# Dummy matrix products on TensorE behind the first transposes and behind the two group sums of a GroupNorm

## What is computed

```
g = x.reshape(B, R, C, 32, 6)
xn = (g - mean(g, (1, 2, 4))) / sqrt(var(g, (1, 2, 4)) + 1e-5)
q0 = xn[:, 0]                                   # first row of each column
sw = softmax over rows of (q0 Wq_s) . (xn Wk_s)
Q = (xn Wq) * scaling * sw ; K = xn Wk ; V = xn Wv
attn = softmax over columns of sum over rows of Q . K
out = x + sum over columns of attn * V
```

## Time and profile before

| | |
|---|---|
| median of 3 runs | 629.26 us (626.15 to 629.93) |
| the profiled execution | 631.34 us, span 629.5 us |
| busy: PE, DVE | 505.7 us (80%), 422.6 us (67%) |
| busy: ACT, POOL | 252.1 us (40%), 225.3 us (36%) |
| mean granted clock of PE | 0.904 |
| DMA | 152.84 MB, mean 243 GB/s |

### The profile page before, as it was taken

The page is one execution under the profiler, slowest core; times in us unless marked ns, Lnnn a source line. Parts: engine busy times, 40 slices in busy tenths (PEclk is TensorE's granted clock), DMA queues, the critical chain, the costliest instruction groups (busy, mean ns, idle before and its releaser), DMA issues.

```text
span 629.5 us, 15205 instructions
## 1 busy us (share of the span) xinstructions
PE 505.7 (80%) x5368; PEld 403.9 (64%) x5368; DVE 422.6 (67%) x1029; ACT 252.1 (40%) x555; POOL 225.3 (36%) x231
## 2 busy tenths in 40 slices
PE   0030198999649999999998999869499997999794
PEld 0020177998525555555546998758399997998683
DVE  2899848699945766767663666846266663667764
ACT  0030136678416666666652113223255652122232
POOL 1010024478503433434341000547166663001484
PEclk9996557799659999999998999979699998999988
DMA  8993004699965998989999999999878757999998
GB/s 275 407 434 163 0 1 118 190 265 273 265 199 165 247 279 247 265 259 246 264 230 194 283 293 279 284 331 263 276 228 263 255 162 158 298 288 283 298 257 227
DMA packets 206876, 152.84 MB, mean 243 GB/s; under 512 B 169648, under 2 KB 189680, under 8 KB 206064
## 3 DMA queue, kind: packets, MB, share of 16 engines
q1 hardware_dynamic: 154912, 132.14, 72.1%
q10 hardware_dynamic: 51920, 20.11, 12.6%
HBM read 95.60 MB, written 56.62 MB: 242 GB/s over the span
## 4 chain that ended last, share of the span: by engine, by line
PE 58%; DVE 18%; DMA 7%; SPq 5%; issue 4%; ACTq 3%; ACT 2%; POOL 2%; POOLq 0%; DVEq 0%
PE PS L990 19%; PE PS L1000 10%; PE PS L1051 7%; DVE EXTRA L603 7%; DVE BIG L849 5%; PE PS L882 3%; PE PS L1080 3%; PE PS L1081 3%; PE PS L1084 3%; PE PS L1082 3%; PE PS L1083 3%; PE PS L921 2%; DMA v_scratch<-EXTRA 2%; DVE EXTRA L709 2%; ACTq L575 2%
## 5 line engine op out<-in xcount | busy, mean ns | idle before, releaser
L449 POOL TENSOR_TENSOR BIG<-EXTRA,BIG 128x192 f32 (+1 forms) x144 | 106.7, 742 | 148.7 <-ACT BIG L519 147.1
L990 PE MATMUL PS<-WP,EXTRA 128*128 128x384 f16 (+1 forms) x1152 | 152.0, 291 | 9.5 <-DMA EXTRA<-xt_scratch 8.7
L990 PEld LDWEIGHTS PS<-WP,EXTRA 128*128 128x128 f16 x1152 | 103.0, 99 | 55.7 <-issue 11.0
L773 DVE TENSOR_TENSOR EXTRA<-PS,SW 128x192 f32<-128x192 f32 x192 | 63.8, 353 | 93.1 <-ACT BIG L534 56.1
L1051 PE MATMUL PS<-BIG,EXTRA 128*128 128x256 f16 x768 | 90.2, 281 | 11.3 <-ACT EXTRA L581 11.2
L457 POOL TENSOR_TENSOR BIG<-BIG,EXTRA 64x512 f32<-64x512 f32 x36 | 45.1, 1265 | 137.0 <-DVE BIG L849 109.0
L1051 PEld LDWEIGHTS PS<-BIG,EXTRA 128*128 128x128 f16 x768 | 76.4, 101 | 24.2 <-issue 10.7
L1000 PE MATMUL PS<-WP,EXTRA 64*128 64x384 f16 (+1 forms) x1152 | 78.0, 285 | 1.1 <-ACT SW L514 1.0
L440 POOL TENSOR_TENSOR BIG<-EXTRA,BIG 128x1024 f16<-128x1024 f32 x24 | 52.7, 2199 | 72.4 <-ACT BIG L490 72.3
L530 ACT CAST EXTRA<-PS 128x384 f16<-128x384 f32 x96 | 46.2, 481 | 54.4 <-PE PS L1000 25.6
L1000 PEld LDWEIGHTS PS<-WP,EXTRA 64*128 64x128 f16 x1152 | 50.0, 95 | 26.7 <-issue 10.0
(11 more groups left out here) (150 smaller groups left out, 692.2 us busy)
## 6 DMA issues: line engine op xcount, KB each, us to landing
EXTRA<-xt_scratch SPq DMA_DIRECT2D x48, 512.0 KB, 3.8
BIG<-in_x SPq DMA_DIRECT2D x6, 3072.0 KB, 21.1
xt_scratch<-BIG SPq DMA_DIRECT2D x48, 256.0 KB, 4.4
EXTRA<-xt_scratch SPq DMA_DIRECT2D x48, 256.0 KB, 4.0
v_scratch<-EXTRA SPq DMA_DIRECT2D x32, 384.0 KB, 4.4
BIG<-v_scratch SPq DMA_DIRECT2D x16, 768.0 KB, 6.6
BIG<-in_x SPq DMA_DIRECT2D x12, 768.0 KB, 9.6
out_x<-BIG ACTq DMA_DIRECT2D x12, 768.0 KB, 7.5
```

Source lines behind the costliest of these rows:

```text
L449: pool.tensor_tensor(QA[:, :, bass.ds(SI[h] * n + low, SI[h])], TQ[h][g % 4], QA[:, :, bass.ds(SI[h] * n, SI[h])], ALU.subtract).then_inc( ...
L773: ins = v.tensor_tensor(tq[:, :, :, i:i + 2], pq.rearrange("p i (m d) -> p m d i", d=D), swv[:, :, i:i + 2].unsqueeze(2).to_broadcast([P, ...
L990: ins = mm(po, xs0, WP[:, w, 0, wc], start=opens and i < 2 and j == 0, stop=not opens and j == 2, skip_group_check=True)
```

## The change

PE gets 60 f32 products that nobody reads. Each multiplies the 128 by 128 unit matrix `ident` (stationary) by its own first 64 columns (moving) into columns 448 to 511 of bank 7. 44 of them stand behind the transposes of block 1, after a new wait for the last chunk of x; 8 stand behind each of the two group sums. No other engine's program is changed.

```diff
             x_transposes(0)
             x_transposes(1)
 
+            def keep_awake(n):
+
+                for _ in range(n):
+                    mm(PS[:, 7, 448:512], ident[:, :], ident[:, 0:64], start=True, stop=True)
+
+            pe.wait_ge(s_x[NXC - 1], 16)
+            keep_awake(44)
             pe.wait_ge(s_st1, 1)
             mm(GS[:, 0, :], ones[:, :], s1, start=True, stop=True).then_inc(s_mm1, 1)
+            keep_awake(8)
             pe.wait_ge(s_st2, 1)
             mm(GS[:, 1, :], ones[:, :], s2, start=True, stop=True).then_inc(s_mm2, 1)
+            keep_awake(8)
 
             pe.wait_ge(s_ab, 1)
```

## The result

The changed kernel took 636.25 us (median of 4 runs, 633.87 to 636.66) against 629.6 us before (4 runs, 626.15 to 631.16). The ratio is 1.0096, with a 95% interval of 1.0066 to 1.0126, so about 6 us slower (4 to 8). Forecast were 634.7 us and a range of 627 to 641.

The account below looks back on a forecast made before the run. DVE's bn_stats bound the kernel up to 69 us, then PE and DVE in turns, mostly PE to 131, then DVE, and SP from 154. 4.1 + 0.75 + 0.6 = +5.4 on 629.26 gave 634.7 us, range 627 to 641.

Parts of the forecast that it names:

- The price of a product: On PE, one dummy product costs two f32 weight loads of 0.213 us, 0.427 us at the low clock.
- The rival of products that don't overlap: Each dummy product waits for the one before to end: 0.64 us each, +18.7 us, end at 648; chance 0.14.
- The clock: During the dummy products PE's clock stays at 0.50 (1.2 GHz), since a busy PE alone does not raise it.
- The rivals in which it rises: Clock rises during the 44: lost again, end at 630.6, chance 0.12; or kept into scoring, 621, chance 0.12.
- rival C: Clock rises and stays up into the scoring stage, with rounds of 4.6 us: -8 us, end at 621; chance 0.12.
- First sum: 44 products from 55.1 us end at 73.9, past the first group sum's old start at 69.77: +4.1 us.
- Between the sums: From first to second group sum PE needs 3.84 us with 8 products, instead of 3.09: +0.75 us.
- To the transposes of scale and shift: Behind the second group sum, 3.84 us instead of 3.22: +0.6 us, with at most +0.1 of drain.
- The row queries: They run at the same low clock and duration as before, starting 5 to 6 us later.
- the price from which the loss passes 6.3 us: Product price above which the kernel is slower by more than 1%, put at 0.445 us.
- Passed on in full: All stages behind the group sums start from them, so a delay there reaches the end undiminished.
- The noise: Where the clock rises in the score-vector rounds may shift, zero to three fast rounds: 2 or 3 us either way.

Follow-up runs that it names:

- front and rounds: Wide products instead of the changed kernel's 60: 54, 10, 10, 6 up to the score vectors, plus 4 in each round of blocks 2 to 6; 630.66 us, ratio 1.0006.
- blocks 8 to 12: Added to front and rounds: 20 wide products before the first projection and 4 more in each of these blocks; 627.79 us, ratio 0.9948 against the kernel before.
- logits: Added to front and rounds: 20 wide products before the first projection and 12 before each of the two logits stages; 623.4 us, ratio 0.9887 against before.
- The two parts by themselves: Changed kernel without the two groups of 8: 635.45 us, ratio 1.0091; changed kernel without the 44 and their wait: 631.87 us, ratio 1.0044.
- the front alone: Wide products instead of the changed kernel's 60: 54 behind x's loads, 10 behind each sum, 6 behind the row queries; 628.81 us; with 20 before the projection, 627.14.

## Why the prediction was right

**The price of a product.** Forecast: 0.427 us at the low clock, with the loads back to back. The trace after has 44 in 73.40 - 54.57 = 18.83 us, 0.428 each. The experiment with wide products shows what makes the price: twice the moving pass and the same loads cost the same at the low clock (eight products of 128 columns take 3.55 us, from 69.89 to 73.44 us, 0.44 each). In its fast part the 47 matmuls of 60 to 65 us make 0.106 us each. The rival of products that don't overlap (0.64) is out. So is the price of 0.107 us per load that the Trainium skill gives (TensorE: Matmul & The Clock Gate, section LDWEIGHTS): at 1.2 GHz an f32 load of 128 columns takes 0.214 here.

**The clock.** Forecast: it stays at 0.50. It did, from 55 to 82 us without a break. What was argued from L921 and the transposes alone is shown by the wide products: with as many loads on the same rows the clock rises. The rivals in which it rises were wrong for the narrow products and right for wide ones; the rise was, however, not worth the 8 us that rival C gave it, since with the clock mostly high through the front and the rounds (mean 0.91 in 80 to 120 us) the time was that of before. Two steps of rival C fail in the traces. A round at the high clock takes 5.0 us and not 4.6, because DVE then leads. And the gain is not kept in the blocks behind the rounds, where PE leads: it loses the clock there (4.56 us a block instead of 3.15), or, where more products hold the clock, these products take the time (4.05 us a block). Behind them DVE and then, after short stretches of ACT and POOL, SP's issues of the stores lead the chain in the traces of all four kernels read here (before, front and rounds, blocks 8 to 12, logits). No run changed those engines' work, so what they give back is read from the chains and was not tested.

**The parts of the sum.** First sum: forecast +4.1; in the trace 73.40 - 69.77 = +3.6, and +4.1 against DVE, whose statistics ended 0.5 us earlier in this execution. Between the sums: forecast 3.84, measured 3.84. To the transposes of scale and shift: 3.84 and up to 0.1 of drain, measured 3.98. The row queries start 5.15 us later than before, 5.6 against DVE, for a forecast of 5.4 to 5.5. The two parts by themselves, 4.2 and 1.4 forecast, measured 3.7 to 7.9 and 1.1 to 4.4. Two slips in the working change nothing: the price from which the loss passes 6.3 us is 0.440 by its own formula and not 0.445, and DVE has five steps between the sums and not four.

**Passed on in full.** The first projection starts at 189.3 instead of 184.3, so in these two executions nothing of the delay was absorbed in the scoring stage. One pair alone would not show this, since that stage varies by as much from one execution to the next; the ratio of all runs, 4 to 8 us slower, agrees with it. At the end the spans differ by 4.7 us and the medians by 6.6; the traces differ by some tenths to 1.5 us in the later stages, by where the clock is lost and comes back there.

**The noise.** Forecast: 2 or 3 us either way. The 29 runs of before spread from 623.5 to 634.3, rather 5 either way; one execution of the kernel with 30 products gained some 4.5 us in the scoring stage alone. The range covered the result, but its width was argued from three runs that spread less than the kernel does. That the median came within 1.6 us of the forecast is in part luck, since single executions scatter by more than that. Some 0.3 us of the 1.6 are the start of the sum (629.26 was taken, and 629.6 measured in the comparison); no run here assigns the rest.

**Open.** Why the 20 products before the projection were worth 5 us behind front and rounds, none that could be measured by themselves, and about 2 behind the front alone, is not settled: the intervals of these kernels are 3 to 5 us wide. The traces show 1.9 us of it: with the 20, the transposes and the first twelve matmuls of the projection take 0.88 and 2.11 us (front, rounds, blocks 8 to 12), without them 1.51 and 3.34 (front and rounds). What is shown is that the combinations with the 20 are faster than before: 0.9887 and 0.9915 clearly, 0.9948 and 0.995 by some 0.2% at the upper end of their intervals, which is too little to build on.

## What to carry to other kernels

Filler work on an engine is free only while the engine ends before the one that leads: work out its length at the clock at which it will really run, and put no fixed number where the wait's length is not fixed. Take dummy products of a kind that stands before a rise of the clock in the kernel's own trace, and look at the granted clock afterwards; a busy PE is no sign of a high one. A held clock pays where PE leads behind it; where another engine is close behind, the gain becomes a wait, and in the wait the clock can be lost again. Products in a stretch that PE itself leads cost their own length, at the high clock too (0.9 us for four here).

## What the hardware showed beyond that

- An f32 product with a stationary operand of 128 by 128 costs two loads of 0.214 us at 1.2 GHz, whether the moving side has 32, 64 or 128 columns. With 64 it is 0.428 us each; a group sum with 32 and eight with 64 take 3.84 us together (77.24 - 73.40); four with 128 take 1.71 us in the chain of the kernel with products in blocks 8 to 12, from 84.67 us on, at 0.50.
- The clock rises in runs of transposes too, as in the 24 of the changed kernel, which are at 0.50 from 118.88 to 121 us and end at 1.00; the mean of 0.56 in 120 to 123.8 puts the rise near 123.3. 24 at the low clock took 5.38 us, 12 at the high one take 1.51:

```profile
118.88 4.99 PE L882 MATMUL PS<-ident,BIG 128*128 128x128 f32 x24
```

The Trainium skill (TensorE: Matmul & The Clock Gate, Part 4: PE-mode transpose) says that the full clock does not engage for transposes; its figures there are for bf16. Here it does, for f32.

- The clock that PE has won in a wait is lost in the next: with wide products it was at 1.00 in 60 to 65 us and at 0.50 in 70 to 75, with 2.75 us idle between.
